# Summing the equal tokens of a pair by two float32r products instead of one float32 product

## The reference, cut to what matters

```python
x_ec = xf[tok_ec]
g = jax.nn.silu(jnp.einsum('ech,ehi->eci', x_ec, w_gate))
u = jnp.einsum('ech,ehi->eci', x_ec, w_up)
y = jnp.einsum('eci,eih->ech', g * u, w_down)
contrib = (y * w_ec[..., None]).reshape(-1, h)
combined = jnp.zeros_like(xf).at[tok_ec.reshape(-1)].add(contrib)
sg = jax.nn.silu(xf @ w_sh_gate)
su = xf @ w_sh_up
combined = combined + sg * su @ w_sh_down
```

## Time and profile before

| what | value |
|---|---|
| time, median of 3 runs | 785.37 us (783.97 to 785.43) |
| the profiled execution's own time | 783.37 us |
| its span, first to last instruction | 781.3 us |
| mean granted TensorE clock | 0.973 |
| busy share: TensorE, VectorE, ScalarE, GpSimd | 92%, 42%, 19%, 29% |
| TensorE line 1492 (gate and up), 1024 records | 172.2 us busy |
| TensorE line 1476 (merge), 64 records | 34.3 us busy, 617 ns each |
| VectorE line 1198 (`same`), 32 | 13.1 us busy, 410 ns each |
| ScalarE line 809 (`y`), 32 | 19.1 us busy, 598 ns each |

### The profile page before, as it was taken

How to read it: one execution, slowest core, us unless ns; L and a number is a source line. 1 busy time by engine, 2 the same in 40 slices (tenths; PEclk the granted TensorE clock), 3 DMA queues, 4 the chain that set the end, 5 groups by cost and what they waited for, 6 DMA issues and landing times.

```text
span 781.3 us, 9943 instructions
## 1 busy us (share of the span) xinstructions
PE 716.6 (92%) x3229; PEld 435.9 (56%) x3229; DVE 328.4 (42%) x839; ACT 151.8 (19%) x244; POOL 225.7 (29%) x234
## 2 busy tenths in 40 slices
PE   2999997799999888999999999999999999998883
PEld 1799977689988744444444444444444444443331
DVE  5887489568777762222222222222222222223220
ACT  5722223232111301111111101111111111111100
POOL 5446464134547122021111221221212212212111
PEclk9999999599999799999999999999999999999997
DMA  8110018300049993999999999999999999999942
GB/s 308 49 50 5 1 55 273 131 0 1 13 137 410 410 337 120 331 322 369 352 359 379 367 329 392 354 355 393 334 356 376 368 388 334 366 379 377 394 109 27
DMA packets 78883, 203.35 MB, mean 260 GB/s; under 512 B 9299, under 2 KB 9427, under 8 KB 78336
## 3 DMA queue, kind: packets, MB, share of 16 engines
q1 hardware_dynamic: 46592, 123.89, 42.1%
q10 hardware_dynamic: 23184, 57.42, 19.1%
q0 software_dynamic: 9072, 21.59, 12.1%
HBM read 178.92 MB, written 24.12 MB: 260 GB/s over the span
## 4 chain that ended last, share of the span: by engine, by line
PE 75%; DVE 14%; issue 2%; ACT 1%; POOL 0%; ACTq 0%; DVEq 0%; POOLq 0%
PE bank L1492 22%; PE bank L1513 11%; PE bank L1280 10%; PE bank L1413 9%; PE bank L1430 5%; PE bank L1476 4%; PE bank L1302 4%; PE bank L1503 3%; PE bank L1442 2%; PE bank L1470 2%; DVE gu L1135 1%; DVE guT L1140 1%; PE bank L1403 1%; DVE key L1010 1%; PE bank L1327 1%
## 5 line engine op out<-in xcount | busy, mean ns | idle before, releaser
L1492 PE MATMUL bank<-w_sb,xT 128*64 128x384 f32 x1024 | 172.2, 489 | 0.0
L580 POOL DMA_INDIRECT out_dram<-ym,midx x32 | 51.5, 1608 | 329.0 <-issue 181.1
L1492 PEld LDWEIGHTS bank<-w_sb,xT 128*64 128x64 f32 x1024 | 70.7, 137 | 102.3 <-issue 101.9
L1135 DVE TENSOR_TENSOR gu<-sg,bank 128x384 f32<-128x384 f32 x48 | 26.5, 553 | 191.1 <-PE bank L1492 133.8
L1513 PE MATMUL bank<-w_sb,guT 128*64 128x512 f32 x384 | 89.5, 601 | 12.3 <-DVE guT L1140 12.3
L1413 PE MATMUL bank<-sh_sb,xS 128*128 128x384 f32 x208 | 69.2, 486 | 0.0
L1193 DVE TENSOR_SCALAR shared_tok<-bank,tok_col 64x64 f32<-64x64 f32 x32 | 9.3, 291 | 121.5 <-PE bank L1470 116.2
L1513 PEld LDWEIGHTS bank<-w_sb,guT 128*64 128x64 f32 x384 | 24.7, 136 | 62.4 <-issue 46.4
L797 ACT ACTIVATE sg<-bank 128x384 f32<-128x384 f32 x48 | 23.6, 492 | 155.5 <-PE bank L1492 77.1
L1413 PEld LDWEIGHTS bank<-sh_sb,xS 128*128 128x128 f32 x208 | 38.5, 190 | 24.1
L1430 PE MATMUL bank<-sh_sb,guT 128*128 128x512 f32 x96 | 45.3, 607 | 0.6 <-ACT guT L832 0.6
(11 more groups left out here) (182 smaller groups left out, 1195.1 us busy)
## 6 DMA issues: line engine op xcount, KB each, us to landing
w_sb<-in_L_ffn_w_gate SPq DMA_DIRECT2D x128, 384.0 KB
w_sb<-in_L_ffn_w_up SPq DMA_DIRECT2D x128, 384.0 KB
w_sb<-in_L_ffn_w_down ACTq DMA_DIRECT2D x116, 384.0 KB
w_sb<-in_L_ffn_w_down SPq DMA_DIRECT2D x12, 384.0 KB
ring<-in_L_attn_x SPq DMA_DIRECT2D x14, 256.0 KB, 3.4
xS<-xt_dram SPq DMA_DIRECT2D x13, 256.0 KB, 7.9
xt_dram<-xwT ACTq DMA_DIRECT2D x12, 256.0 KB, 3.4
out_dram<-yS POOLq DMA_DIRECT2D x4, 768.0 KB
```

The lines of the kernel that those rows point to most:

```text
L580: pool.indirect_dma_start(out=out[:, :], out_offset=bass.IndirectOffsetOnAxis(ap=midx[r][u][:, :], axis=0), in_=ym[u][:, :], in_offset=Non ...
L1135: dve.tensor_tensor(gu[n][:, :], sg[n][:, :], ps_u[u][:, 0:I], ALU.mult).then_inc(gu_ready[n], 1)
L1492: ins = pe.matmul(ps[e * C:(e + 1) * C, 0:I], xT[u][:, c, e * C:(e + 1) * C], gate_up(r, u, e, w)[:, c, :], start=(c == 0), stop=(c == KC ...
```

## The change

`y` becomes two tiles, a high part `y_hi` in float32r and a low part `y_lo`. ScalarE writes `y_hi` from the down product scaled by `wcol`, so its instruction gets a scale operand of one value per row. VectorE gets a new step `low_part`: it waits for `y_hi`, computes down product times `wcol` minus `y_hi`, and writes `y_lo`. The matrix `same` no longer carries the weights, and is made of zeros and ones in float32r. `merge_pair` waits for `y_low` instead of `y_out` and makes two float32r products that add up in PSUM. For `u` = 0 `low_part` stands ahead of `same_tokens(j, 1)`; for `u` = 1 it stands at the head of VectorE's next group, ahead of line 1203.

```diff
@@ -184,9 +184,11 @@
         sg, gu = ([tile(f"{name}{n}", [P, I], at=None if n < 2 else xw_at + i * I * 4) for n in range(3)]
                   for i, name in enumerate(("sg", "gu")))
         guT = [tile(f"guT{n}", [P, IC, P], at=None if n < 2 else st_at + 2048) for n in range(3)]
-        y = [tile(f"y{u}", [P, D]) for u in range(2)]
+        y_hi = [tile(f"y_hi{u}", [P, D], F32R) for u in range(2)]
+        y_lo = [tile(f"y_lo{u}", [P, D], F32R, at=xin_at + 2048 + u * 2048) for u in range(2)]
+        assert xn_at == xin_at + K4
         ym = [tile(f"ym{u}", [P, D]) for u in range(2)]
-        same = [tile(f"same{u}", [P, P]) for u in range(2)]
+        same = [tile(f"same{u}", [P, P], F32R) for u in range(2)]
         shared_tok = tile("shared_tok", [P, C])
         yS = tile("yS", [P, 3, D], at=vx_at)
         assert st_at == vx_at + K4
@@ -294,7 +296,7 @@
         g_ready, u_ready, sg_ready, gu_ready, gu_turned, guT_ready, d_ready = (
             [sem(f"{n}{u}") for u in range(3)]
             for n in ("g_ready", "u_ready", "sg_ready", "gu_ready", "gu_turned", "guT_ready", "d_ready"))
-        y_out, ym_ready, yS_ready = sem2("y_out"), sem2("ym_ready"), sem("yS_ready")
+        y_out, y_low, ym_ready, yS_ready = sem2("y_out"), sem2("y_low"), sem2("ym_ready"), sem("yS_ready")
         tok_col_ready, tok_row_ready = sem2("tok_col_ready"), sem2("tok_row_ready")
         same_ready, midx_ready, m_ready = sem2("same_ready"), sem2("midx_ready"), sem2("m_ready")
         pair_tok_ready = sem("pair_tok_ready")
@@ -806,7 +808,8 @@
                 def pair_out(u):
                     act.wait_ge(d_ready[u], j + 1)
                     need(act, m_ready[u], j)
-                    act.activation(y[u][:, :], ps_d[0][:, :], ACT.Copy).then_inc(y_out[u], 1)
+                    act.wait_ge(wcol_ready[u], j + 1)
+                    act.activation(y_hi[u][:, :], ps_d[0][:, :], ACT.Copy, scale=wcol[r][u][:, :]).then_inc(y_out[u], 1)
                     if left > u:
                         fill_matrix(act, j + 1 + u, (r + 1 + u) % 3, 1 - u, 2)
 
@@ -1194,11 +1197,18 @@
                 seq.then(dve.tensor_reduce(twice[C:P, :], shared_tok[C:P, :], AX.X, ALU.max))
                 dve.scalar_tensor_tensor(out=midx[r][u][:, :], in0=twice[:, :], scalar=float(TOKENS), in1=tok_col[u][:, :],
                                          op0=ALU.mult, op1=ALU.add).then_inc(midx_ready[u], 1)
+                dve.tensor_scalar(same[u][:, :], ps_tok[:, :], tok_col[u][:, :], None, ALU.is_equal).then_inc(same_ready[u], 1)
+
+            def low_part(j, r, u):
+                dve.wait_ge(y_out[u], j + 1)
                 dve.wait_ge(wcol_ready[u], j + 1)
-                dve.tensor_scalar(same[u][:, :], ps_tok[:, :], tok_col[u][:, :], wcol[r][u][:, :],
-                                  ALU.is_equal, ALU.mult).then_inc(same_ready[u], 1)
+                dve.scalar_tensor_tensor(out=y_lo[u][:, :], in0=ps_d[0][:, :], scalar=wcol[r][u][:, :],
+                                         in1=y_hi[u][:, :].bitcast(F32), op0=ALU.mult,
+                                         op1=ALU.subtract).then_inc(y_low[u], 1)
 
             def group(j, thirds, r, shared=True, first=False):
+                if not first:
+                    low_part(j - 1, (r + 2) % 3, 1)
                 for u in range(2):
                     dve.tensor_copy(tok_col[u][:, :], pair_tok[:, bass.ds(j * 2 + u, 1)]).then_inc(tok_col_ready[u], 1)
                     dve.wait_ge(xg_full[r][u], thirds * 16 + 16)
@@ -1214,6 +1224,7 @@
                 if shared:
                     turn_copy(j + LEAD, 2, ps_xt)
                 turn_copy(j, 0, ps_ht)
+                low_part(j, r, 0)
                 dve.wait_ge(tok_col_ready[1], j + 1)
                 same_tokens(j, r, 1)
                 merged_out(j, thirds, r, 0)
@@ -1233,6 +1244,7 @@
             seq.base, seq.n = 0, before + per * (SHARED - 4)
             for j in range(SHARED - 1, GROUPS):
                 group(j, j // 3, j % 3, shared=j < SHARED)
+            low_part(GROUPS - 1, (GROUPS - 1) % 3, 1)
             merged_out(GROUPS - 1, (GROUPS - 1) // 3, (GROUPS - 1) % 3, 1)
 
 
@@ -1472,8 +1484,9 @@
 
             def merge_pair(j, u):
                 pe.wait_ge(same_ready[u], j + 1)
-                pe.wait_ge(y_out[u], j + 1)
-                pe.matmul(ps_d[0][:, :], same[u][:, :], y[u][:, :], start=True, stop=True).then_inc(m_ready[u], 1)
+                pe.wait_ge(y_low[u], j + 1)
+                pe.matmul(ps_d[0][:, :], same[u][:, :], y_hi[u][:, :], start=True, stop=False)
+                pe.matmul(ps_d[0][:, :], same[u][:, :], y_lo[u][:, :], start=False, stop=True).then_inc(m_ready[u], 1)
 
             def group(j, thirds, r, last=False, shared=True, first=False):
                 shared_done = j + (LEAD + 1) if shared else SHARED + LEAD
```

## The result

| | before | after |
|---|---|---|
| time, median | 784.67 us (783.91 to 785.43, 4 runs) | 816.05 us (812.4 to 816.44, 4 runs) |
| span of the profiled execution | 781.3 us | 814.4 us |
| ratio after / before, 95% interval | | 1.0395 (1.0372 to 1.0418) |

The change makes the kernel 4.0% slower. The new low part is line 1205. In the kernels of the experiments lines can stand a few further up or down. In the traces a float32 product of 128x512 is two records of TensorE, a float32r product one; "behind" a step means later in an engine's order.

What follows compares the result with a forecast made beforehand. The expert stage was taken as one long queue on TensorE. Group starts 25.5, even merges 5.1, odd merges -5.8 and -1.4, last merge 0.4 give +23.8 on 785.4: 809.2 us, eight-in-ten range 803.5 to 816.

Steps and rivals of the forecast that it cites:

- slow low parts: Rival: VectorE's low part runs at line 1071's long time, up to 841 us, or 820 for a third of pairs; chance 0.04.
- a stretch of the stage at half clock: Sign of being wrong: part of the expert stage at half clock, where 1.00 was forecast.
- start of a group: At 15 group starts TensorE idles while the tok_col copy waits behind the low part: 1.70 us each, +25.5.
- even merge: At 16 even pairs' merges, waiting for the low part outweighs the cheaper product: +0.32 us each, +5.1.
- odd merge: At 15 odd pairs' merges the low part is ready and float32r is cheaper: -0.48 us each, -5.8 and -1.4.
- last merge: At the final merge, ScalarE's start to VectorE's copy goes from 1.88 to 2.29 us, +0.4.
- the price of the hand-over: At the even merge, VectorE's low part to TensorE's start takes 0.05 us.
- the second float32r product: At the even merge, from the second float32r product to the gate product takes 0.24 us.
- The clock: Rival: new pauses at 15 group starts make the granted clock fall, 37 us in all, to 847; chance 0.03.
- No wait for weights: Rival: transfers are the true bound, TensorE waits for a pair's weights, total stays some 785.8 us; chance 0.03.
- float32r did give its gain: Rival: float32r saves nothing in the merges; odd +7.2, even +7.7, total 824 us; chance 0.02.
- The estimate of 0.69 for the low part: Skill-page formula for VectorE's low part, 0.69 us; the forecast used a measured row instead; by the page about 1.6 us less.

Runs made afterwards that it cites:

- The run with three products: The changed kernel with both low parts moved under other products and each merge's low product made twice: 774.78 us, ratio 0.9869.
- the first experiment: The changed kernel with the odd pair's low part behind the next group's tok_col and wcol copies and same_tokens(j, 0): 785.65 us, ratio 1.0023.
- the wait alone: The kernel before, with VectorE waiting for the odd pair's y ahead of each group's tok_col copy, no low part or float32r: 802.28 us, ratio 1.0225.
- the fastest kernel: The changed kernel with odd low part and even merge moved later, and gated(j, 0, 0) ahead of merged_out(j-1, 1) in the last three groups: 761.09 us.

## Why the prediction was right, point by point

The direction, the mechanism and its place were right, the size too small: 809.2 was forecast, and 816.05 lies on the range's upper end, which was written as 816. That the range reaches so far was luck: its own terms ended at 813.5 (809.2 + 4.0 gives 813.2), and it was drawn on to 816 for slow low parts, which didn't occur. One of the prediction's own signs of being wrong did appear, a stretch of the stage at half clock, and a group without a shared tile took 27.4 us where it had 25.6. The profiled execution's span grew by 33.1 us, and its terms can be read off:

| term | forecast | measured in the trace |
|---|---|---|
| start of a group, 15 times | 25.5 (1.70 each) | 25.7 (12 of 1.70, 3 of 1.78) |
| even merge, 16 times | 5.1 (0.32) | 7.7 (0.48) |
| odd merge, 12 + 3 times | -7.2 (-0.48) | -5.9 (-0.39) |
| last merge | 0.4 | 0.5 |
| slow down products, 3 times | 0, a rival | 4.6 |
| start of the stage | 0 | 0.7 |
| a wait of 0.41 that is gone, in group 12 | 0 | -0.4 |
| sum | 23.8 | 32.9 |

The measured terms come to 32.9 of a growth of 33.1. The wait in group 12 is TensorE's for the odd pair's `gated`: 0.41 us at 692.93 in the kernel before, 0.04 at the same place after. The median grew by 31.4, as the profiled execution of before was 1.3 us below its median and that of after 0.4 above.

**Start of a group.** Right in place, chain and size. ScalarE's copy with a scale took 0.69 as reckoned, the low part 0.75 (0.74 reckoned), the hand-over to VectorE 0.03. The copy of `tok_col` reached TensorE after 0.06 at twelve starts (0.05 reckoned) and after 0.14 at three, which is the 0.2 in the sum.

**The even merge: mis-sized.** The step that failed is the price of the hand-over and of the second product. From the low part's end at 579.39 to TensorE's weight load at 579.51 it is 0.12, where 0.05 was taken from the hand-over of `gated` to line 1503. And the second float32r product was priced from a row whose successor is again float32r; here its successor is the float32 gate product, and it takes 0.33 (579.85 to 580.18) where 0.24 was reckoned. Together 0.16 each, 2.6 us.

**The odd merge: mis-sized by the same.** 0.56 instead of 0.48 for the pair of products, as the last one again stands ahead of the gate product (339.39 to 339.72, 0.33). The run with three products shows that it is a fixed part, not the price of a product: one more costs 0.23.

**The clock: the rival that was partly right, and the largest term missing.** It had a chance of 0.03 and 37 us, put on all 15 starts; the text argued that the groups without a shared tile have 2.6 us idle and hold 1.00. What failed is this step: it took the old idle time, of one execution, as proof for a place where the new pause is added to it, and put the term at nothing. In those three groups the clock fell each time, for one down product, 1.5 to 1.6 us each, 4.6 in all. At the twelve other starts it did not.

**The rivals that fell.** No wait for weights appears, so the transfers were not the bound. The low part was never slow: 0.75 us over 32. float32r did give its gain. That VectorE executes in its order (the rule cited from the Trainium skill, TensorE: Matmul & The Clock Gate, section on the array's architectural detail) is what the first experiment shows from the other side: moving one line on that queue took back 30.4 us. The estimate of 0.69 for the low part, by the formula of the Trainium skill, VectorE: DVE Perf Modes, section on the TRN2 errata, was below the measured 0.75.

## What to carry to other kernels

When a cheaper product needs a new operand from another engine, look first at what is queued behind the new step on that engine, and at who waits for that: here a copy of 0.15 us, moved behind a step it has nothing to do with, cost 26 us. A float32r pair for one float32 product is worth its 0.4 us each only if its split lies under other work; with the same arithmetic and three moves of order, the same idea went from 4% slower to 3% faster. One of these moves, the even merge's, was worth 4.5 us in float32, too. And a product moved into a gap in which its engine waits anyway costs only what it is longer than the gap.

## What the runs showed of the hardware that was not expected

- A pause of 1.5 to 1.6 us, followed 7 to 8 us later by waits of 1.24 and 0.65, preceded a fall of the granted clock from 1.00 (2.4 GHz) for one down product, which took 4.3 to 4.5 us in place of 2.8, at 0.50 (1.2 GHz) for most of it. This happened in all nine such places of three kernels' traces, whether the merge was float32 or float32r. With the pause but without the 1.24 it happened in none of three; with the waits but without the pause it was none of three in the kernel before and in the first edit, one of three in three others, two of three in the float32 kernel with the even merge moved; with the shorter pause of the wait alone, one of three; with neither the pause nor the 1.24, none of three in the fastest kernel. So the pause isn't needed, but with it and both waits the clock fell at nine of nine places, with the waits alone at five of eighteen. What decides there stays open.
- The clock is a part of the spread between runs: the changed kernel's runs with mean clocks of 0.963 to 0.967 took 815.9 to 816.4 us, the one with 0.970 took 812.4. A mean doesn't say where the clock fell. The part ahead of the expert stage, which no edit touches, varies as well: over the twelve traces the stage's first product of the token numbers starts at 299.7 to 304.2 us, and in the four traces with 302.9 or more the clock was once more at 0.50, between 176 and 177 us, where it was 1.00 in the others.
- The low float32r product of a merge cost 0.33 to the start of the float32 gate product behind it, but 0.23 to another float32r product and 0.23 to the turns of tokens, which are float32 but a single record each (559.77 to 560.00). So a float32 successor alone doesn't explain the 0.33. Why, no run here shows.
